# Norms for images 1 to 3 made within the first image's layer 0 scans instead of in a block of their own

## The chip, the cores and the metric

The kernel runs on one core of one Trainium2 chip. The metric is the device time of one execution in microseconds (us), median over several runs. The core has five engines with an instruction stream each: TensorE (PE in the profile; its weight loads are PEld), VectorE (DVE), ScalarE (ACT), GpSimd (POOL), and SyncE (SP), which here only issues DMAs. Each stream is in a fixed order; the engines signal to each other with semaphores. SBUF is the on-chip memory, PSUM the eight banks (128 partitions by 512 float32 each) into which TensorE writes.

## The reference

The input is x of shape (4, 384, 32, 32): four images, 384 channels, 1024 positions. Two layers follow, each a scan block and a feed-forward block, with residuals. What matters here is the beginning of layer 0, cut to its core:

```python
def _ln_c(v, eps=1e-6):                      # over the 384 channels, no scale or bias
    m = jnp.mean(v, axis=1, keepdims=True)
    s = jnp.var(v, axis=1, keepdims=True)
    return (v - m) / jnp.sqrt(s + eps)

x = x + L0_conv(_ln_c(x))                    # then the feed-forward, then layer 1

# L0_conv: four directions k (as is, turned, and both reversed), 384 channels, 16 states
dts, Bs, Cs = split(einsum('bkdl,kcd->bkcl', cross_scan(x), x_proj_weight))
dt = softplus(dt_projs_weight @ dts + bias)
h  = h * exp(dt * A) + dt * u * B            # along the 1024 positions, for each channel and state
y  = sum over states of h * C
# y + D u, directions summed, layer norm, gelu
```

## The kernel before, in words

Everything is float32. An image lies in SBUF as 128 partitions by 3 tiles by 1024 positions. Image 0 is worked alone first: its norm (`layer_norm`, L165), its layer 0 scans (`lane_scans`), and so on. The scans of images 1 to 3 begin later, and read their normed input from a DRAM tensor, `normed`. That tensor is filled by `norms_ahead` (L248 to L322), a block of its own between the norm of image 0 and its scans. It loads three images, and takes them in six halves of 512 positions. For each half TensorE sums over channels with a matrix of 1/384 (`mean_mat`), VectorE subtracts the mean, ScalarE squares, TensorE sums the squares, ScalarE makes the inverse root by Ln and Exp, and VectorE multiplies all three tiles with it (L300). SyncE stores each image. A block ends with a barrier of all engines: the scans can't begin before the last store has landed.

`lane_scans` works 12 lanes for image 0: 4 directions by 3 tiles of 128 channels. A lane has 16 steps, one for each state n. In step s the engines do this:

- ScalarE `decay` (L534): exp(delta * A) of 128 x 1024 into one of two PSUM slots (`slot(s)`, banks 2-3 or 4-5). It waits until VectorE is done with that slot, so for the product of step s-2 (or its scan).
- GpSimd `drive` (L574): du * B, up to two steps ahead of the scan.
- VectorE `scan` (L609): the recurrence over 1024 positions; it waits for decay and drive of its own step.
- the product with C: VectorE `weigh` (L618) for 11 of the 16 steps, GpSimd (L581) for n = 1, 4, 7, 10, 13 (`by_pool`), two steps later.
- TensorE `add` (L476): sums the products over n in banks 0-1 with an identity matrix. For n % 3 = 1 the add comes two steps late.

Once in each lane there is more. TensorE makes the dt product of the next lane at n = 7 (L461, banks 6-7), ScalarE turns it to softplus in three pieces at n = 10, 11, 12 (L514, L518, L522), VectorE makes `delta` at n = 12 (L597), and GpSimd `du` at n = 14 (L565). At n = 1 VectorE takes the finished sum of the lane before out of banks 0-1 (`take`: L2275, L2279 or L2283), and the first add of the new lane waits for that. When the direction changes, a projection (L450) and ScalarE's copies of it (L507) come within the last lane of a direction, with stores and loads of the B and C rows. Banks 6-7 (`WORK`) are free in the other lanes from n = 0 to n = 6. SyncE loads B rows four steps ahead (L398).

The order on each engine is written out by hand: the loop over s calls these pieces at the numbers n in the tables at the head of `lane_scans`. Nothing reorders them.

Of the kernel before, what the change touches and what calls it, by code (L numbers as in the profile page):

```python
# [17 lines left out]
ALU = mybir.AluOpType  # L18
# [8 lines left out]
P = 128  # L27
# [77 lines left out]
def load_weights(p, m, st, image):  # L105

    nc, io = p.nc, p.io
    with nc.Block() as block:
# [21 lines left out]
        def _(eng):  # L130
            eng.memset(m.eps5[:, :], 1e-5).then_inc(st.own, 1)
            eng.memset(m.eps6[:, :], 1e-6).then_inc(st.own, 1)
            eng.wait_ge(st.small, 16 * 6)

# [113 lines left out]
def norms_ahead(p, m, st, images, tiles, normed, sq, rstd, eps):  # L248


    nc, ps = p.nc, m.ps
    HALVES = len(images) * NH

    def half(j):
        return tiles[j // NH], cols(j % NH)

    with nc.Block() as block:
        @block.sync
        def _(eng):
            p.clear_last(eng, st)  # L260
            for i, x in enumerate(images):
                eng.dma_start(tiles[i], x).then_inc(st.loaded[i], 16)
            for i in range(len(images)):
                eng.wait_ge(st.normed, (i + 1) * NH)
                eng.dma_start(normed[i], tiles[i]).then_inc(st.stored, 16)
            eng.wait_ge(st.stored, 16 * len(images))

        @block.tensor
        def _(eng):
            for j in range(HALVES + 1):  # L270
                if j < HALVES:
                    t, at = half(j)
                    eng.wait_ge(st.loaded[j // NH], 16)
                    if j >= 4:
                        eng.wait_ge(st.centred, (j - 3) * CT)
                    for k in range(CT):
                        mm = eng.matmul(ps[:, j % 4, :], m.mean_mat[:, :], t[:, k, at], start=k == 0, stop=k == CT - 1)
                    mm.then_inc(st.mean, 1)
                if j:
                    v = j - 1  # L280
                    if v >= 4:
                        eng.wait_ge(st.logged, v - 3)
                    for k in range(CT):
                        eng.wait_ge(st.squared, v * CT + k + 1)
                        mm = eng.matmul(ps[:, 4 + v % 4, :], m.mean_mat[:, :], sq[:, k, cols(v % 2)], start=k == 0,
                                        stop=k == CT - 1)
                    mm.then_inc(st.variance, 1)

        @block.vector
        def _(eng):  # L290
            for j in range(HALVES + 1):
                if j < HALVES:
                    t, at = half(j)
                    eng.wait_ge(st.mean, j + 1)
                    for k in range(CT):
                        eng.tensor_tensor(t[:, k, at], t[:, k, at], ps[:, j % 4, :], ALU.subtract).then_inc(st.centred, 1)
                if j:
                    t, at = half(j - 1)
                    eng.wait_ge(st.rstd, j)
                    eng.tensor_tensor(t[:, :, at], t[:, :, at], over_tiles(rstd[:, cols((j - 1) % 2)]),  # L300
                                      ALU.mult).then_inc(st.normed, 1)

        @block.scalar
        def _(eng):
            eng.preload_act_table_set(EXP_LN)
            for j in range(HALVES + 1):
                if j < HALVES:
                    t, at = half(j)
                    if j >= 2:
                        eng.wait_ge(st.variance, j - 1)  # L310
                    for k in range(CT):
                        eng.wait_ge(st.centred, j * CT + k + 1)
                        eng.activation(sq[:, k, cols(j % 2)], t[:, k, at], ACT.Square).then_inc(st.squared, 1)
                if j:
                    v = j - 1
                    if v >= 2:
                        eng.wait_ge(st.normed, v - 1)
                    r = rstd[:, cols(v % 2)]
                    eng.wait_ge(st.variance, v + 1)
                    eng.activation(r, ps[:, 4 + v % 4, :], ACT.Ln, bias=eps[:, :]).then_inc(st.logged, 1)  # L320
                    eng.wait_ge(st.logged, v + 1)
                    eng.activation(r, r, ACT.Exp, scale=-0.5).then_inc(st.rstd, 1)  # L322


def lane_scans(p, m, st, directions, lanes, rows, turn=None, load_ahead=None):
# [17 lines left out]
    C_LATE = {1: (6,), 3: (7,)}  # L343
    prods = [m.prod[:, 0, :], m.prod[:, 1, :]]
# [38 lines left out]
    with nc.Block() as block:  # L383
        @block.sync
        def _(eng):
# [24 lines left out]

            store_rows(0)
# [6 lines left out]
            for s in range(STEPS):  # L418
                i, n = s // N, s % N
                if s + BRING < STEPS:  # L420
                    load_b(s + BRING)
                d = lanes[i].direction
# [14 lines left out]
            if load_ahead is not None:  # L437
                eng.wait_ge(st.loaded, 16)

        @block.tensor  # L440
        def _(eng):
            def project(i, c):
                d = lanes[i].direction
                x = directions[d]
                if x.turned:
                    eng.wait_ge(st.turned, CT)
                if i:
                    eng.wait_ge(st.delta, i)
                for k, src in enumerate(x.kts):
                    mm = eng.matmul(ps[0:BC + x.rank, WORK + c, :], x.wx(k), src[:, cols(c)], start=k == 0,  # L450
                                    stop=k == len(x.kts) - 1)
                mm.then_inc(st.projected, 1)

            def dt_product(i):
                x = directions[lanes[i].direction]
                eng.wait_ge(st.low, (lanes[i].direction + 1) * NH)
                if i:
                    eng.wait_ge(st.delta, i)
                a = lanes[i].dt_at
# [23 lines left out]
            for s in range(STEPS):  # L483
# [5 lines left out]
                if fresh(i + 1) and n in PROJECT_AT:  # L489
                    project(i + 1, PROJECT_AT.index(n))  # L490
                if n == DT_AT and i + 1 < len(lanes):
                    dt_product(i + 1)

        @block.scalar
        def _(eng):
            eng.preload_act_table_set(EXP_LN)

# [44 lines left out]
            for s in range(STEPS):  # L542
# [6 lines left out]
                if fresh(i + 1) and n in LOW_AT:  # L549
                    take_projection(i + 1, LOW_AT.index(n))  # L550
                if i + 1 < len(lanes):
# [40 lines left out]
        def _(eng):  # L592
# [26 lines left out]

            def take(i):  # L620
# [6 lines left out]
            for s in range(STEPS):  # L627
# [4 lines left out]
                if n == TAKE_AT and i:  # L632
                    take(i - 1)
                if n == DELTA_AT and i + 1 < len(lanes):
# [1564 lines left out]
def build(nc, io, out, rows, half_rows, normed, gates):  # L2199
    with ExitStack() as ctx:  # L2200
# [4 lines left out]
                ("x", [P, CT, L], F32), ("vec", [P, VEC_N], F32), ("ident", [P, P], F32), ("mean_mat", [P, P], F32),  # L2205
                ("eps5", [P, 1], F32), ("eps6", [P, 1], F32), ("Dsum", [P, CT], F32),
# [4 lines left out]
        def stage(name, *signals):  # L2211
# [21 lines left out]
        s_ahead = stage("ahead", "mean", "centred", "squared", "variance", "logged", "rstd", "normed", "stored",  # L2233
                        *(f"loaded{i}" for i in range(B - 1)))
        s_ahead.loaded = [s_ahead[f"loaded{i}"] for i in range(B - 1)]
# [15 lines left out]
        with ExitStack() as conv:  # L2251
# [19 lines left out]
            def first_image():  # L2271
# [9 lines left out]
                def take_turned(j):  # L2281
# [5 lines left out]
                norms_ahead(p, m, s_ahead, [io["x"][i] for i in range(1, B)], [m.h[:, :, :], ys, un], [normed[i] for i in range(1, B)],  # L2287
                            m.prod, rstd, m.eps6)
# [10 lines left out]
                with ExitStack() as scans:  # L2299
                    lane_scans(p, scan_tensors(scans, "first"), s_scan, directions, lanes, rows, turn=(u, ut))  # L2300
# [253 lines left out]
```

## Time and profile before

| | |
|---|---|
| time, median of 3 runs | 5902.71 us (5900.35 to 5903.08) |
| the profiled execution's own time | 5910.61 us, its span 5908.1 us |
| PE, DVE, ACT, POOL busy over the span | 82%, 79%, 58%, 69% |
| mean granted TensorE clock | 0.914 of full speed |
| norm of image 0, last operation ends | 30.4 us |
| block `norms_ahead` and its barrier | 30.7 to 81.5 us |
| scans of image 0 | 81.5 to about 752 us |
| the rest (layers for images 0 to 3) | about 752 to 5908 us |

All times within the trace are in us from the start of the span. A timeline row gives start, duration, engine, line, operation, and in brackets how long the engine had been idle and what ended that. Several instructions in a run are merged into one row with a count (x4). One float32 `matmul` of the kernel is two MATMUL records in the trace: the add of a step (two matmuls) is x4, a mean of a half (three matmuls) x6.

### The profile page before, as it was taken

What the parts mean: (1) busy time and instruction counts of PE and PEld (TensorE: products, weight loads), DVE (VectorE), ACT (ScalarE), POOL (GpSimd) and SP (SyncE); (2) the same over time, 40 slices, a digit from 0 to 9 for tenths busy, and PEclk for the clock granted to TensorE, in tenths of its full rate; (3) what the DMA queues carried; (4) which work ended last, traced back from release to release, by engine and by line L of the source; (5) the groups of instructions that cost most, each with busy time, mean ns of one, the idle gap of its engine ahead of it and who ended that gap; (6) DMA issues with size and microseconds to landing.
All of it is one profiled execution on the core that took longest, in us unless ns stands there. A gap on an engine that the chain in (4) does not pass through costs nothing. (4 is left out here: it accounts for less than half of the span.)

```text
span 5908.1 us, 66280 instructions
## 1 busy us (share of the span) xinstructions
PE 4843.1 (82%) x20263; PEld 3285.0 (56%) x20263; DVE 4666.1 (79%) x5015; ACT 3401.0 (58%) x5199; POOL 4054.7 (69%) x2861
## 2 busy tenths in 40 slices
PE   5777786778888897778888888778888988777998
PEld 2222242246666745656666645665766764664787
DVE  5999947969999948977999956895999984896544
ACT  3433353337777756656777756664777765664222
POOL 3999917948888817865888844893888871884121
PEclk8898898889999998888999998888999999888999
DMA  5555405428777605636777723653877761662110
GB/s 210 211 214 196 167 20 196 157 97 285 266 249 269 231 26 208 215 127 219 255 269 244 271 100 139 206 190 123 276 252 267 250 203 41 211 217 86 49 49 27
DMA packets 340470, 1076.86 MB, mean 182 GB/s; under 512 B 31522, under 2 KB 123266, under 8 KB 332808
## 3 DMA queue, kind: packets, MB, share of 16 engines
q1 hardware_dynamic: 340104, 1072.52, 52.4%
q8 instruction: 163, 2.67, 0.2%
q14 instruction: 203, 1.66, 0.1%
HBM read 1058.72 MB, written 13.68 MB: 182 GB/s over the span
## 5 line engine op out<-in xcount | busy, mean ns | idle before, releaser
L940 PE MATMUL banks<-ident,prod 128*128 128x128 f32 x4752 | 799.7, 295 | 581.8 <-DVE prod L1154 494.4
L940 PEld LDWEIGHTS banks<-ident,prod 128*128 128x128 f32 x4752 | 570.8, 149 | 906.6 <-DVE prod L1154 764.3
L476 PE MATMUL banks<-prod,ident 128*128 128x512 f32 x972 | 567.5, 725 | 299.3 <-DVE prod L618 234.6
L1141 DVE TENSOR_TENSOR_SCAN banks<-banks,h 128x512 f32<-128x512 f32 x594 | 725.7, 1222 | 99.6 <-POOL h L1092 69.4
L1092 POOL TENSOR_TENSOR h<-lane,Bb 128x512 f32<-128x512 f32 x576 | 722.5, 1273 | 51.3 <-DMA Bb<-half_rows 46.7
L1033 ACT ACTIVATE banks<-lane,A 128x512 f32<-128x512 f32 x864 | 579.5, 685 | 217.6 <-DVE prod L1154 95.2
L534 ACT ACTIVATE banks<-delta_first,A 128x1024 f32<-128x1024 f32 x288 | 321.8, 1118 | 577.2 <-DVE prod L618 479.0
L1154 DVE TENSOR_TENSOR prod<-banks,half_C_a 128x512 f32<-128x512 f32 x792 | 548.1, 692 | 98.5 <-DVE banks L1141 3.9
L1101 POOL TENSOR_TENSOR h<-h,half_C_a 128x512 f32<-128x512 f32 x360 | 461.9, 1283 | 217.4 <-DVE half_carry_a L1146 149.5
L476 PEld LDWEIGHTS banks<-prod,ident 128*128 128x128 f32 x972 | 197.1, 220 | 661.8 <-DVE prod L618 405.2
L974 PE MATMUL banks<-Cb,w_a 128*128 128x256 f32 x2304 | 552.4, 380 | 2.3 <-ACT Cb L1046 2.3
L1141 DVE TENSOR_TENSOR_SCAN banks<-banks,half_carry_a,h 128x512 f32<-128x512 f32 x396 | 506.1, 1278 | 6.6 <-POOL h L1092 3.5
L1092 POOL TENSOR_TENSOR h<-half_du_a,Bb 128x512 f32<-128x512 f32 x384 | 482.2, 1273 | 17.0 <-DMA Bb<-half_rows 15.3
L1033 ACT ACTIVATE banks<-half_delta_a,A 128x512 f32<-128x512 f32 x576 | 383.5, 684 | 161.4 <-DVE prod L1154 81.9
L609 DVE TENSOR_TENSOR_SCAN banks<-banks,h 128x1024 f32<-128x1024 f32 x198 | 453.4, 2290 | 28.0 <-POOL h L574 26.3
L961 PE MATMUL banks<-big,w_a 128*128 128x256 f32 x1728 | 443.4, 400 | 1.5 <-DMA w_a<-w_in 1.0
L974 PEld LDWEIGHTS banks<-Cb,w_a 128*128 128x128 f32 x2304 | 412.1, 190 | 45.3 <-ACT Cb L1046 3.2
L1092 POOL TENSOR_TENSOR h<-lane,Cb 128x512 f32<-128x512 f32 x288 | 364.9, 1280 | 15.9 <-DVE banks L1141 15.1
L1046 ACT ACT_TABLE_LOAD x288 | 369.5, 1283 | 5.1
L1073 ACT ACT_TABLE_LOAD x288 | 369.5, 1283 | 5.1
L574 POOL TENSOR_TENSOR h<-du_first,Cb 128x1024 f32<-128x1024 f32 x144 | 337.9, 2352 | 46.6 <-DVE h L609 21.4
L961 PEld LDWEIGHTS banks<-big,w_a 128*128 128x128 f32 x1728 | 331.3, 201 | 54.6 <-issue 11.6
(382 smaller groups left out, 10971.2 us busy)
## 6 DMA issues: line engine op xcount, KB each, us to landing
Bb<-half_rows SPq DMA_DIRECT2D x576, 512.0 KB, 4.4
Cb<-half_rows SPq DMA_DIRECT2D x288, 512.0 KB, 4.5
w_a<-w_in SPq DMA_DIRECT2D x256, 576.0 KB, 6.5
half_C_a<-half_rows SPq DMA_DIRECT2D x160, 512.0 KB, 6.6
Bb<-rows SPq DMA_DIRECT2D x144, 512.0 KB, 4.4
Cb<-rows SPq DMA_DIRECT2D x144, 512.0 KB, 4.1
w_b<-w_in SPq DMA_DIRECT2D x128, 576.0 KB, 6.4
C_first<-rows SPq DMA_DIRECT2D x40, 1024.0 KB, 8.3
```

What stands on the lines that cost most here:

```text
L476: mm = eng.matmul(ps[:, c, :], m.ident[:, :], src[:, cols(c)], start=n == 0, stop=added(s) == (i + 1) * N, skip_group_check=True)
L609: eng.tensor_tensor_scan(flip(to), flip(slot(s)), flip(m.dBu[:, s % DRIVES, :]), 0.0, ALU.mult, ALU.add).then_inc(st.scanned, 1)
L940: mm = eng.matmul(ps[:, 0, at], src[:, at], m.ident[:, :], start=n == 0 and k == 0, stop=added(s) == (i + 1) * N, is_transpose=True, skip_ ...
L961: mm = eng.matmul(hidden(u), g.w1[:, w % WRING, k, t * P:(t + 1) * P], g.un[:, k, at], start=k == 0, stop=k == CT - 1, skip_group_check=True)
L974: mm = eng.matmul(total(f), g.w2[:, w % WRING, t, f * P:(f + 1) * P], g.h[:, u % HRING, :], start=u % PER == 0 and f != 1, stop=u % PER == ...
L1033: eng.activation(slot(s), m.delta[i % 2], ACT.Exp, scale=x.A(j, n)).then_inc(st.decay, 1)
L1046: eng.activation(g.h[:, u % HRING, :], hidden(u), ACT.Gelu, bias=m.vec[:, b:b + 1]).then_inc(st.gelu, 1)
L1073: eng.preload_act_table_set(EXP_LN)
L1092: eng.tensor_tensor(m.dBu[:, s % DRIVES, :], m.du[i % 2], m.B[b % BRING][:, cols(s % 2)], ALU.mult).then_inc(st.dbu, 1)
L1101: eng.tensor_tensor(h, h, m.C[:, s % N, :], ALU.mult).then_inc(st.pooled, 1)
L1141: eng.tensor_tensor_scan(flip(to), flip(slot(s)), flip(m.dBu[:, s % DRIVES, :]), initial, ALU.mult, ALU.add).then_inc(st.scanned, 1)
L1154: eng.tensor_tensor(prods[own(s) % PRODS], slot(s), m.C[:, n, :], ALU.mult).then_inc(st.prod, 1)
```

## The change

The block `norms_ahead` is gone, and `lane_scans` gets the same work for image 0's lanes. Six of the twelve lanes, those with i = 1, 3, 4, 6, 7, 9, take one half of an image each (`norm_of`). The half is loaded into `raw` (half of the tile `un`); centring is no longer a mean on TensorE and a subtraction on VectorE, but a product with I - M and -M (`less_mean`, `minus_mean`, made once at the start of the program) that sums x minus its mean in a WORK bank. ScalarE copies it to `centred`, squares it into `raw`, and makes the inverse root; VectorE multiplies; SyncE stores. `centre` runs at n = 0, 1, 3 on TensorE, the copies at n = 1, 2, 4 and the squares at n = 4, 5, 5 on ScalarE, `variance` at n = 6 on TensorE, `inverse_root` at n = 7 on ScalarE, `normalize` at n = 9 on VectorE, and the store and the next load at n = 11 on SyncE.

```diff
+            eng.tensor_scalar(m.minus_mean[:, :], m.mean_mat[:, :], -1.0, None, ALU.mult).then_inc(st.own, 1)
+            eng.tensor_tensor(m.less_mean[:, :], m.ident[:, :], m.mean_mat[:, :], ALU.subtract).then_inc(st.own, 1)
...
-def norms_ahead(p, m, st, images, tiles, normed, sq, rstd, eps):
...
+    CENTRE_AT, CENTRED_AT, SQUARE_AT, VARIANCE_AT, RSTD_AT, NORM_AT, STORE_NORM_AT = (0, 1, 3), (1, 2, 4), (4, 5, 5), 6, 7, 9, 11
+    norm_of = {}
+    if norms is not None:
+        lanes_between = [i for i in range(1, len(lanes)) if (i + 1) % CT]
+        norm_of = {i: j for j, i in enumerate(lanes_between[:NH * len(norms.x)])}
+        raw, centred = norms.tile[:, :, cols(0)], norms.tile[:, :, cols(1)]
+        squares, rstd = raw, norms.tile[:, 0, cols(0)]
...
+            def load_x(j):
+                if j:
+                    eng.wait_ge(norms.st.normed, j)
+                eng.dma_start(raw, norms.x[j // NH][:, :, cols(j % NH)]).then_inc(norms.st.loaded, 16)
+
+            def store_norm(j):
+                eng.wait_ge(norms.st.normed, j + 1)
+                eng.dma_start(norms.to[j // NH][:, :, cols(j % NH)], centred).then_inc(norms.st.stored, 16)
...
+                if norm_of and i == 0 and n == N - 1:
+                    load_x(0)
+                if i in norm_of and n == STORE_NORM_AT:
+                    store_norm(norm_of[i])
+                    if norm_of[i] + 1 < len(norm_of):
+                        load_x(norm_of[i] + 1)
...
+            def centre(i, k):
+                j = norm_of[i]
+                if k == 0:
+                    eng.wait_ge(st.delta, i + 1)
+                    eng.wait_ge(norms.st.loaded, 16 * (j + 1))
+                if k == 2:
+                    eng.wait_ge(norms.st.centred, j * CT + 1)
+                for q in range(CT):
+                    mm = eng.matmul(ps[:, WORK + k % 2, :], (m.less_mean if q == k else m.minus_mean)[:, :], raw[:, q, :],
+                                    start=q == 0, stop=q == CT - 1)
+                mm.then_inc(norms.st.product, 1)
+
+            def variance(i):
+                j = norm_of[i]
+                for k in range(CT):
+                    eng.wait_ge(norms.st.squared, j * CT + k + 1)
+                    mm = eng.matmul(ps[:, WORK + 1, :], m.mean_mat[:, :], squares[:, k, :], start=k == 0, stop=k == CT - 1)
+                mm.then_inc(norms.st.variance, 1)
...
+                if i - 1 in norm_of:
+                    eng.wait_ge(norms.st.logged, norm_of[i - 1] + 1)
...
+                if i in norm_of and n in CENTRE_AT:
+                    centre(i, CENTRE_AT.index(n))
+                if i in norm_of and n == VARIANCE_AT:
+                    variance(i)
...
+            def take_centred(i, k):
+                j = norm_of[i]
+                if k == 0 and j:
+                    eng.wait_ge(norms.st.stored, 16 * j)
+                eng.wait_ge(norms.st.product, j * CT + k + 1)
+                eng.activation(centred[:, k, :], ps[:, WORK + k % 2, :], ACT.Copy).then_inc(norms.st.centred, 1)
+
+            def square(i, k):
+                j = norm_of[i]
+                eng.wait_ge(norms.st.centred, j * CT + k + 1)
+                eng.wait_ge(norms.st.product, (j + 1) * CT)
+                eng.activation(squares[:, k, :], centred[:, k, :], ACT.Square).then_inc(norms.st.squared, 1)
+
+            def inverse_root(i):
+                j = norm_of[i]
+                eng.wait_ge(norms.st.variance, j + 1)
+                eng.activation(rstd, ps[:, WORK + 1, :], ACT.Ln, bias=m.eps6[:, :]).then_inc(norms.st.logged, 1)
+                eng.wait_ge(norms.st.logged, j + 1)
+                eng.activation(rstd, rstd, ACT.Exp, scale=-0.5).then_inc(norms.st.rstd, 1)
...
+                if i in norm_of and n in CENTRED_AT:
+                    take_centred(i, CENTRED_AT.index(n))
+                if i in norm_of:
+                    for k in range(CT):
+                        if n == SQUARE_AT[k]:
+                            square(i, k)
+                if i in norm_of and n == RSTD_AT:
+                    inverse_root(i)
...
+            def normalize(i):
+                j = norm_of[i]
+                eng.wait_ge(norms.st.rstd, j + 1)
+                eng.wait_ge(norms.st.centred, (j + 1) * CT)
+                eng.tensor_tensor(centred, centred, over_tiles(rstd), ALU.mult).then_inc(norms.st.normed, 1)
...
+                if i in norm_of and n == NORM_AT:
+                    normalize(i)
...
-                norms_ahead(p, m, s_ahead, [io["x"][i] for i in range(1, B)], [m.h[:, :, :], ys, un], [normed[i] for i in range(1, B)],
-                            m.prod, rstd, m.eps6)
...
+                    norms = Named(st=s_ahead, tile=un, x=[io["x"][i] for i in range(1, B)], to=[normed[i] for i in range(1, B)])
+                    lane_scans(p, scan_tensors(scans, "first"), s_scan, directions, lanes, rows, turn=(u, ut), norms=norms)
+                p.last = Named(all=s_scan.all + s_ahead.all)
```

ScalarE before, from the end of lane 0 to the end of lane 1 (L534 is the decay, L547 a turned copy, L514 and L518 the next lane's softplus):

```order
L534 ACTIVATE banks<-delta_first,A 128x1024 x2
L547 ACTIVATE big<-big 128x1024
L534 ACTIVATE banks<-delta_first,A 128x1024 x12
L514 ACTIVATE du_first<-banks 128x1024
L534 ACTIVATE banks<-delta_first,A 128x1024
L518 ACTIVATE du_first<-du_first 128x1024
```

ScalarE now, lane 1 from its second decay on (L532 is the decay, L481 the copy of a centred tile, L487 the square, L492 and L494 Ln and Exp of the inverse root):

```order
L481 ACTIVATE big<-banks 128x512
L532 ACTIVATE banks<-delta_first,A 128x1024
L481 ACTIVATE big<-banks 128x512
L532 ACTIVATE banks<-delta_first,A 128x1024 x2
L481 ACTIVATE big<-banks 128x512
L487 ACTIVATE big<-big 128x512
L532 ACTIVATE banks<-delta_first,A 128x1024
L487 ACTIVATE big<-big 128x512 x2
L532 ACTIVATE banks<-delta_first,A 128x1024 x2
L492 ACTIVATE big<-banks,eps 128x512
L494 ACTIVATE big<-big 128x512
L532 ACTIVATE banks<-delta_first,A 128x1024 x3
```

The twelve decays in a row (n = 15 of lane 0, then n = 0 to 10 of lane 1) have become three ahead of the first row shown, then one, two, one, two and three, with the copies, squares and the inverse root between them.

TensorE before, from a late add of lane 0 through the dt product that lane 1 makes for lane 2 (L476 is the add, L461 the dt product):

```order
L476 MATMUL banks<-h,ident 128x512 x2
L476 MATMUL banks<-prod,ident 128x512 x12
L476 MATMUL banks<-h,ident 128x512 x2
L461 MATMUL banks<-lane,lowk 128x512 x2
L476 MATMUL banks<-prod,ident 128x512 x10
L476 MATMUL banks<-h,ident 128x512 x2
```

TensorE now, from the first add of lane 1 to its dt product (L450 is the add, L403 the centring, L411 the sum of squares, L435 the dt product):

```order
L450 MATMUL banks<-prod,ident 128x512 x2
L403 MATMUL banks<-big,less_mean 128x512
L403 MATMUL banks<-big,minus_mean 128x512 x3
L403 MATMUL banks<-big,less_mean 128x512
L403 MATMUL banks<-big,minus_mean 128x512
L450 MATMUL banks<-prod,ident 128x512 x6
L403 MATMUL banks<-big,minus_mean 128x512 x2
L403 MATMUL banks<-big,less_mean 128x512
L450 MATMUL banks<-prod,ident 128x512 x4
L450 MATMUL banks<-h,ident 128x512 x2
L411 MATMUL banks<-big,mean_mat 128x512 x3
L435 MATMUL banks<-lane,lowk 128x512 x2
```

The first two centrings (six matmuls) stand behind the first add of the lane, the third behind the adds of n = 2, 3 and 1, and the sum of squares behind the adds of n = 5, 6 and 4 and ahead of the dt product.

## Rows read from the trace of the kernel before

**Rows 1.** `windows`: stretch; us; busy of PE, PEld, DVE, ACT, POOL; clock; DMA

```profile
100.40:748.00 647.60, 465.53 (x842) 165.90 (x843) 615.21 (x346) 253.42 (x232) 607.51 (x262) 0.87 0.57 203
```

**Rows 2.** Waits by total, 100 to 740 us: total, times, longest

```profile
ACT banks L534 <- DVE prod L618: 315.8, 125, 6.4
...
DVE banks L609 <- POOL h L574: 16.6, 14, 5.0
```

**Rows 3.** Timeline of VectorE in lane 3, first half

```profile
261.87 2.30 DVE L609 TENSOR_TENSOR_SCAN banks<-banks,h 128x1024 f32<-128x1024 f32 x1 [0.96 <-POOL h L574]
...
267.63 1.26 DVE L2275 SCALAR_TENSOR_TENSOR big<-big,Dsum,banks 128x1024 f32<-128x1024 f32 x1
268.81 2.29 DVE L609 TENSOR_TENSOR_SCAN banks<-banks,h 128x1024 f32<-128x1024 f32 x1
...
274.80 1.23 DVE L618 TENSOR_TENSOR prod<-banks,C_first 128x1024 f32<-128x1024 f32 x1
...
278.13 2.27 DVE L609 TENSOR_TENSOR_SCAN banks<-banks,h 128x1024 f32<-128x1024 f32 x1
...
284.10 1.23 DVE L618 TENSOR_TENSOR prod<-banks,C_first 128x1024 f32<-128x1024 f32 x1
...
287.75 2.30 DVE L609 TENSOR_TENSOR_SCAN banks<-banks,h 128x1024 f32<-128x1024 f32 x1
```

**Rows 4.** Timeline of ScalarE, the decay of n = 2

```profile
265.56 1.12 ACT L534 ACTIVATE banks<-delta_first,A 128x1024 f32<-128x1024 f32 x1 [3.50 <-DVE prod L618]
```

**Rows 5.** Timeline of TensorE in lane 3, first half

```profile
269.04 5.46 PE L476 MATMUL banks<-prod,ident 128*128 128x512 f32 x8 [4.38 <-DVE big L2275]
276.07 3.70 PE L476 MATMUL banks<-prod,ident 128*128 128x512 f32 x8 [1.58 <-DVE prod L618]
...
285.38 2.20 PE L476 MATMUL banks<-prod,ident 128*128 128x512 f32 x4 [0.35 <-DVE prod L618]
287.42 1.88 PE L476 MATMUL banks<-h,ident 128*128 128x512 f32 x4
```

**Rows 6.** Timeline of TensorE, first add of lane 9

```profile
594.25 1.95 PE L476 MATMUL banks<-prod,ident 128*128 128x512 f32 x4 [2.63 <-DVE big L2283]
```

**Rows 7.** Timeline of all engines, the block `norms_ahead` and what follows

```profile
30.69 1.28 ACT L305 ACT_TABLE_LOAD   x1 [2.07 <-PEq L165]
...
44.46 1.82 ACT L313 ACTIVATE prod<-h 128x512 f32<-128x512 f32 x3 [12.49 <-DVE h L296]
...
48.69 2.74 PE L277 MATMUL banks<-big,mean_mat 128*128 128x512 f32 x6
...
48.89 0.69 ACT L320 ACTIVATE Cb<-banks,eps 128x512 f32<-128x512 f32 x1
...
49.61 0.63 ACT L322 ACTIVATE Cb<-Cb 128x512 f32<-128x512 f32 x1
...
50.27 1.76 DVE L300 TENSOR_TENSOR h<-h,Cb 128x1536 f32<-128x1536 f32 x1 [2.07 <-ACT Cb L322]
...
81.52 6.78 PE L450 MATMUL banks<-big,w0x 128*44 128x512 f32 x12 [8.75 <-PEq L257]
81.79 1.28 ACT L496 ACT_TABLE_LOAD   x1 [7.58 <-PEq L257]
```

**Rows 8.** Line L208: count: ns min/median/max, starts; form

```profile
L208 DVE TENSOR_TENSOR un<-un,row_all x2: 1745/2964/4182, 5457.7 to 5461.8; 128x1536 f32<-128x1536 f32 x2
```

**Rows 9.** Timeline of GpSimd around 5457 us

```profile
5455.04 5.20 POOL L1904 TENSOR_TENSOR w_lo<-raw,w_hi 128x1152 fp32r<-128x1152 f32 x2
```

**Rows 10.** Groups by line, GpSimd, 154 to 749 us

```profile
L574 POOL TENSOR_TENSOR h<-du_first,Cb 128x1024 f32<-128x1024 f32 x88 | 206.6, 2353 | 29.6 <-DVE prod L609 13.3 <-DVE h L609 13.1 <-DVE banks L609 2.6
```

**Rows 11.** DMA issues, 30 to 82 us: count, KB each, us to landing

```profile
normed<-big SPq DMA_DIRECT2D x2, 1536.0 KB, 5.1
h<-x_in SPq DMA_DIRECT2D x1, 1536.0 KB, 6.8
```

**Rows 12.** DMA issues, 100 to 740 us

```profile
Bb<-rows SPq DMA_DIRECT2D x94, 512.0 KB, 4.4
```

More of the change, by code:

```diff
@@ L245, in _ @@
                                        scale=m.vec[:, w:w + 1]).then_inc(st.scaled, 1)
-def norms_ahead(p, m, st, images, tiles, normed, sq, rstd, eps):
[L251 to L322, printed above, removed]
@@ L325, in lane_scans @@
-def lane_scans(p, m, st, directions, lanes, rows, turn=None, load_ahead=None):
+def lane_scans(p, m, st, directions, lanes, rows, turn=None, load_ahead=None, norms=None):
     nc, ps, low = p.nc, m.ps, m.low
@@ L438, in _ @@
                 eng.wait_ge(st.loaded, 16)
+            if norm_of:
+                eng.wait_ge(norms.st.stored, 16 * len(norm_of))
         @block.tensor
         def _(eng):
+            def centre(i, k):
[15 more added lines that the diff above has]
+                mm.then_inc(norms.st.variance, 1)
             def project(i, c):
@@ L2205, in build @@
                 ("x", [P, CT, L], F32), ("vec", [P, VEC_N], F32), ("ident", [P, P], F32), ("mean_mat", [P, P], F32),
+                ("minus_mean", [P, P], F32), ("less_mean", [P, P], F32),
                 ("eps5", [P, 1], F32), ("eps6", [P, 1], F32), ("Dsum", [P, CT], F32),
@@ L2232, in build @@
         s_moved = stage("moved", "sent", "reloaded")
-        s_ahead = stage("ahead", "mean", "centred", "squared", "variance", "logged", "rstd", "normed", "stored",
-                        *(f"loaded{i}" for i in range(B - 1)))
-        s_ahead.loaded = [s_ahead[f"loaded{i}"] for i in range(B - 1)]
+        s_ahead = stage("ahead", "loaded", "product", "centred", "squared", "variance", "logged", "rstd", "normed", "stored")
         s_moe = stage("moe", "ones", "got0", "got1", "scores", "step", "exped", "u_high", "u_split", "high", "split", "hidden", "gelu", "h_high", "h_split", "down",
@@ L2299, in first_image @@
                 with ExitStack() as scans:
-                    lane_scans(p, scan_tensors(scans, "first"), s_scan, directions, lanes, rows, turn=(u, ut))
+                    norms = Named(st=s_ahead, tile=un, x=[io["x"][i] for i in range(1, B)], to=[normed[i] for i in range(1, B)])
+                    lane_scans(p, scan_tensors(scans, "first"), s_scan, directions, lanes, rows, turn=(u, ut), norms=norms)
+                p.last = Named(all=s_scan.all + s_ahead.all)
             def half_scan_tensors(stack, name):
```

## The prediction

> **What bounds the kernel now.** I read first the busy shares by stretch, then the list of waits, then the timeline of one lane on each engine, because the change puts work into a loop whose order is fixed. In the scans of image 0 VectorE is busy 615.2 of 647.6 us and GpSimd 607.5; TensorE 465.5, at a mean granted clock of 0.87, and ScalarE 253.4 [rows 1]. So VectorE bounds the stage, with GpSimd just behind, and ScalarE looks as if it had room. The list of waits says what this room is made of: ScalarE stands waiting for VectorE's product 125 times, 315.8 us in all, before a decay [rows 2]. A decay writes into the slot that the product of two steps earlier has just left, and the scan after next needs it. ScalarE can't work ahead, so its idle time can't be filled with work that itself waits for something late. The timeline of lane 3 (starting at 261.87) is my example: the decay of n = 2 starts at 265.56, takes 1.12 [rows 4], and its scan starts at 268.81 [rows 3].
>
> **What goes.** The first instruction of the old block on ScalarE starts at 30.69, the same instruction of the scans at 81.79 [rows 7]. With the block gone the second moves to the place of the first: 51.1 us off. All of it is on the path, because of the barrier and because nothing of the scans ran in it. The block's loads and stores move into the scans.
>
> **What comes: the instructions.** Six lanes (i = 1, 3, 4, 6, 7, 9) get one half of an image each. On TensorE a centring is three matmuls, six passes, like the old mean of a half: 2.74 us [rows 7]; there are three per lane, and one sum of squares of the same size, 11.0 us per lane. On ScalarE: three copies and three squares of 0.61 (1.82 for three), Ln 0.69 and Exp 0.63 [rows 7]: 5.0 us per lane. On VectorE one multiplication, 1.76 [rows 7]; the subtraction is gone. By busy time alone this would cost 1.76 x 6 = 10.6 us on the bound engine. What costs is the order.
>
> **What comes: three waits per lane.** ScalarE works in its written order. A copy at n = 1 stands ahead of the decay of n = 2, and if TensorE's product isn't there the decay waits too, and VectorE behind it. I take each of the three places at which TensorE's result depends on VectorE's latest product, from the rows of lane 3.
>
> Place A, n = 0 to 2. TensorE's first centring stands behind the lane's first add, which waits for the take of the lane before; it starts at 269.04, when the take (267.63 + 1.26) is done. The row is 5.46 for eight passes, against 3.70 for eight at 276.07 [rows 5]: 1.76 more, as if the first four passes had run at 1.2 GHz after an idle time of 4.38. So the add takes 3.4, the centring 2.74, the copy 0.6, the decay 1.12, and 0.1 for signals: the scan of n = 2 starts at 277.0, not 268.81, 8.2 us late. Where TensorE is at 2.4 GHz, as in lane 9 (1.95 for four passes after 2.63 idle [rows 6]), it is 6.5. I counted the lanes' first adds: five of the six are of the slow kind, mean 7.9.
>
> Place B, n = 3 to 5. The product of n = 3 (274.80 + 1.23) releases eight passes at 276.07, two adds. The third centring can issue 3.43 later (eight times 0.43), at 279.5; 2.74, copy 0.6, square 0.6 (it is written ahead of the decay), decay 1.12, signals 0.1: 284.7, and the scan of n = 5 now starts at 278.13 [rows 3, 5]: 6.6 late.
>
> Place C, n = 6 to 8. The product of n = 6 ends at 285.33, the adds of n = 6 and 4 run from 285.38 to 289.3 [rows 3, 5]. Then the sum of squares 2.74, Ln 0.69, Exp 0.63, decay 1.12, signals and gaps 0.2: 294.6, while the scan of n = 8 starts at 287.75 now: 6.8 late.
>
> The three add up, since each chain starts from a VectorE product that comes after the stall before. Could GpSimd hide some? It runs at most two steps ahead of the scan, so it stops with VectorE. 7.9 + 6.6 + 6.8 = 21.3 us per lane. The other new pieces aren't late: the second centring is done before the decay of n = 2 is, and the squares at n = 5 stand ahead of a decay that has a whole scan and product of time.
>
> **Clock.** B and C hold 28 passes, 12 us at 2.4 GHz, and the rows I used have one slow pass between them. At the stage's mean clock of 0.87 [rows 1] they would take 1.8 more; TensorE is idle some 6 us ahead of C. I take 1.0 per lane, between 0 and 1.8.
>
> **The multiplication, and what it meets.** GpSimd is busy with operations of 2.35 [rows 10] nearly all the time. The same multiplication, with both inputs in SBUF, took 4.18 once and 1.75 once at 5457 [rows 8]; the long one began at 5457.7 and ended about when GpSimd's pair did, 5455.04 + 5.20 [rows 9]. So it waits for GpSimd's running operation: between 0 and 2.35, I take 1.2, 3.0 in all. Against this stands a gain: VectorE's 0.96 of waiting for GpSimd at a lane's first scan [rows 3] goes, since GpSimd has caught up. Net 2.0 per lane, 1.76 - 0.96 = 0.8 without the meeting, 4.1 with a full one and no gain.
>
> The Trainium skill has this as a rule: "SBUF — State Buffer", section "SBUF: two separate sides", says that a VectorE operation with two SBUF inputs and a GpSimd operation that reads SBUF exclude each other for the whole instruction. The trace agrees (4.18 beside 1.75). Without the rule one would put 0.8 in the sum, with it about 2.0: 7 us over six lanes. It speaks against the change a little; the inputs of the old subtraction and of the scan lie partly in PSUM, and were not under it.
>
> **DMA.** One store and one load of 768 KB follow each other at n = 11, behind a wait for the multiplication at n = 9. 1536 KB took 5.1 to store and 6.8 to load [rows 11], so the pair is some 6 us. Behind it in SyncE's queue are the B rows, four steps of 3.4 ahead of their use (647.6 us by 12 lanes, 54.0 each, by 16 [rows 1]), so 13 us, landing in 4.4 [rows 12]; 6 + 4.4 is less. Cost 0, and at the other end one step of 3.4 us per lane. The lanes with C loads have no store. The extra semaphores to clear and the two small matrices at the start: 0 to 1 us, taken as 0.5.
>
> **Sum.** Per lane 21.3 + 1.0 + 2.0 = 24.3; six lanes 145.8; + 0.5 - 51.1 = +95. From the profiled execution's 5910.6 that is 6006; the median of the runs shown is 7.9 below that execution, so 5902.7 + 95 = 5998 us, slower by 1.6%.
>
> **Rivals.** Slow clock: if all 34 passes of the three chains that aren't counted slow so far (6 at A, 28 at B and C, 14.6 us) ran at 1.2 GHz, it would be 14.6 instead of 1.0 per lane, +82 us: 6080. For it speaks that the stalls make TensorE's idle times longer than the 4.38 after which it was slow; against it, that eight passes at 276.07 were fast soon after. Half of it gives 6036. 5 in 100 for above 6035.
>
> Only part of the waits binds: if B and C were hidden (because ScalarE's decay turned out to be ahead of the copy, or TensorE ran the centring ahead of the adds) 7.9 + 2.0 = 9.9 per lane, +8 us: 5911. I see nothing in the order that would do it. 3 in 100.
>
> The other side: no wait binds, ScalarE's 315.8 us of waiting swallow all, and only the multiplications cost, 6 x 2.0 = 12: 12 - 51 = -39, 5864 us. It decides at the copy of n = 1: if it ends by 267.7 in lane 3 (268.81 - 1.12), nothing is lost there. Since even at 2.4 GHz TensorE can't begin the centring before 270.7, I give it 3 in 100. That the block is not really on the path, or that the scans stay where they are, would need work in it that the scans share; there is none.
>
> DMA: B rows late by a step in each of six lanes, +20: 6018. 6 in 100, inside the range.
>
> **Range and chances.** The lowest sum of the forecast has every pass at 2.4 GHz (A 6.5, B 6.5, C 6.5), 0.8 for the multiplication, and 1.7 us saved at the first projection, which now runs its first passes slow after 8.75 idle [rows 7]: 6 x 20.3 - 51 - 1.7 = +69, 5972. The highest has half of the slow clock, 6036. I say 5972 to 6035. A measurement of this kernel can tell about 0.2%, 12 us, from no change. Faster by more than that: 3 in 100. Within: 4 in 100. Slower: 93 in 100.
>
> **What would show it.** In the profile after: ScalarE waits for TensorE ahead of the copies of n = 1 and n = 4 and ahead of Ln at n = 7; VectorE's scans of n = 2, 5 and 8 wait for a decay, some 8, 7 and 7 us, in six lanes, and nowhere else; these lanes last about 78 us instead of 54. The multiplication takes over 1.76 where GpSimd is busy. The first scan comes 51 us earlier. I am wrong if these scans start on time, or if lanes with a half last under 70 us.

## The result, and the profile after

The changed kernel takes 6011.5 us in the median (6007.2 to 6016.0, 4 runs), the kernel before 5902.9: a ratio of 1.0181, 95% interval 1.0168 to 1.0194. Five more runs of it, in a later set with its own runs of before, had a median of 6006.25 against 5910.0, ratio 1.0164 (1.0150 to 1.0178). It is slower by 1.6 to 1.8%, where +1.6% was forecast.

The profiled execution lasted 6007.2 us with a span of 6005.4, which is 97.3 more than before. Three marks divide it: the first scan of image 0, the first DMA of the stage behind the scans, and the end.

| profile | first scan starts | scans of image 0 | later stages |
|---|---|---|---|
| before | 100.4 | 652.1 | 5155.6 |
| changed | 47.2 | 803.1 | 5155.1 |
| difference | -53.2 | +151.0 | -0.5 |

The stage of the scans, to hold against [rows 1]:

```profile
47.23:846.10 798.87, 560.85 (x988) 206.12 (x989) 631.40 (x352) 277.83 (x280) 608.95 (x262) 0.83 0.49 177
```

VectorE's busy time is 631.4 against 615.2, which is little for a stage that is 151 longer. The bound engine has become idle. The list of waits from 50 to 800 us (engine and line that waited, what it waited for, total, times, longest), to hold against [rows 2]:

```profile
ACT banks L532 <- DVE prod L624: 226.7, 100, 6.4
...
ACT big L481 <- PE banks L403: 142.3, 18, 14.3
DVE banks L615 <- ACT banks L532: 133.1, 18, 9.1
...
ACT big L492 <- PE banks L411: 55.2, 6, 10.1
...
DVE banks L615 <- POOL h L580: 11.3, 18, 1.0
```

VectorE waited 18 times for a decay, three times in each of six lanes, 133.1 us in all; before there was no such line. ScalarE's own waiting for VectorE's product is down from 315.8 to 226.7, and beside it stand 142.3 for the centred product and 55.2 for the sum of squares. VectorE's waits for GpSimd have hardly changed: the 11.3 here and the 16.6 of [rows 2] differ mainly by the first scan's 4.95, which this window leaves out. Lane 3 on VectorE, against [rows 3]:

```profile
234.04 2.30 DVE L615 TENSOR_TENSOR_SCAN banks<-banks,h 128x1024 f32<-128x1024 f32 x1 [0.95 <-POOL h L580]
...
250.14 2.30 DVE L615 TENSOR_TENSOR_SCAN banks<-banks,h 128x1024 f32<-128x1024 f32 x1 [9.07 <-ACT banks L532]
...
265.89 2.30 DVE L615 TENSOR_TENSOR_SCAN banks<-banks,h 128x1024 f32<-128x1024 f32 x1 [6.33 <-ACT banks L532]
...
282.21 2.30 DVE L615 TENSOR_TENSOR_SCAN banks<-banks,h 128x1024 f32<-128x1024 f32 x1 [6.91 <-ACT banks L532]
...
289.34 2.83 DVE L630 TENSOR_TENSOR big<-big 128x1536 f32<-128x1536 f32 x1
```

The bracket before the scans of n = 2, 5 and 8 reads 9.07, 6.33 and 6.91, and the last row is the multiplication, 2.83. Over the six lanes the three waits average 8.7, 6.5 and 7.0. From first scan to first scan these lanes last 78.9 us on average (77.5 to 81.0), where they lasted 54.0. ScalarE in the same lane, against [rows 4]:

```profile
248.51 0.60 ACT L481 ACTIVATE big<-banks 128x512 f32<-128x512 f32 x1 [14.26 <-PE banks L403]
249.00 1.11 ACT L532 ACTIVATE banks<-delta_first,A 128x1024 f32<-128x1024 f32 x1
...
263.73 0.60 ACT L481 ACTIVATE big<-banks 128x512 f32<-128x512 f32 x1 [8.78 <-PE banks L403]
264.23 0.62 ACT L487 ACTIVATE big<-big 128x512 f32<-128x512 f32 x1
264.74 1.11 ACT L532 ACTIVATE banks<-delta_first,A 128x1024 f32<-128x1024 f32 x1
...
279.82 0.69 ACT L492 ACTIVATE big<-banks,eps 128x512 f32<-128x512 f32 x1 [9.12 <-PE banks L411]
280.54 0.63 ACT L494 ACTIVATE big<-big 128x512 f32<-128x512 f32 x1
281.07 2.14 ACT L532 ACTIVATE banks<-delta_first,A 128x1024 f32<-128x1024 f32 x2
```

Each copy or Ln ends a long wait for TensorE, and a decay (L532) stands right behind it: that decay is the one VectorE waited for. TensorE, against [rows 5]:

```profile
241.22 3.75 PE L450 MATMUL banks<-prod,ident 128*128 128x512 f32 x4 [4.37 <-DVE big L2288]
244.76 1.91 PE L403 MATMUL banks<-big,less_mean 128*128 128x512 f32 x2
246.47 2.80 PE L403 MATMUL banks<-big,minus_mean 128*128 128x512 f32 x6
...
269.60 5.89 PE L450 MATMUL banks<-prod,ident 128*128 128x512 f32 x8 [5.90 <-DVE prod L624]
275.33 1.88 PE L450 MATMUL banks<-h,ident 128*128 128x512 f32 x4
277.04 2.74 PE L411 MATMUL banks<-big,mean_mat 128*128 128x512 f32 x6
```

The first add takes 3.54 us for its four passes (241.22 to 244.76) after 4.37 idle, so it runs at 1.2 GHz, and the first two passes of the centring are slow too (1.71 to 246.47); the next six take 2.63. At 269.60 the add of n = 5 begins after 5.90 us of idleness and is slow again, up into the adds ahead of the sum of squares.

### The profile page after: what moved, and what is told of

Its sections match the earlier page's. It is cut to its first block and busy times, and to the rows that moved or that the text cites. A ratio compares the mean times of both kernels' runs of the same rounds, so it can differ in the third digit from the quotient of the medians.

```text
span 6005.4 us, 66441 instructions
## 1 busy us (share of the span) xinstructions
PE 4899.9 (82%) x20335; PEld 3306.1 (55%) x20335; DVE 4659.0 (78%) x4999; ACT 3406.1 (57%) x5216; POOL 4059.7 (68%) x2861
## 5 line engine op out<-in xcount | busy, mean ns | idle before, releaser
L450 PE MATMUL banks<-prod,ident 128*128 128x512 f32 x972 | 601.2, 764 | 346.6 <-DVE prod L624 277.7
L450 PEld LDWEIGHTS banks<-prod,ident 128*128 128x128 f32 x972 | 209.5, 235 | 728.5 <-DVE prod L624 457.2
L532 ACT ACTIVATE banks<-delta_first,A 128x1024 f32<-128x1024 f32 x288 | 321.0, 1116 | 507.1 <-DVE prod L624 412.2
L615 DVE TENSOR_TENSOR_SCAN banks<-banks,h 128x1024 f32<-128x1024 f32 x198 | 453.3, 2289 | 160.6 <-ACT banks L532 133.1
L580 POOL TENSOR_TENSOR h<-du_first,Bb 128x1024 f32<-128x1024 f32 x144 | 337.4, 2351 | 96.3 <-DVE banks L615 59.2
```

What stands on the lines that cost most here:

```text
L450: mm = eng.matmul(ps[:, c, :], m.ident[:, :], src[:, cols(c)], start=n == 0, stop=added(s) == (i + 1) * N, skip_group_check=True)
L580: eng.tensor_tensor(m.dBu[:, s % DRIVES, :], m.du[:, i % 2, :], m.B[s % BRING], ALU.mult).then_inc(st.dbu, 1)
L615: eng.tensor_tensor_scan(flip(to), flip(slot(s)), flip(m.dBu[:, s % DRIVES, :]), 0.0, ALU.mult, ALU.add).then_inc(st.scanned, 1)
```

## The experiments

Stage times are from each kernel's profile, as in the table above. e1 to e4 and e5 to e8 were timed in two sets, each beside its own runs of before (medians 5906.55 and 5910.03), so across the sets the ratios compare better than the medians.

| kernel | median us | ratio to before, 95% | first scan | scans | later |
|---|---|---|---|---|---|
| e1 no norms | 5864.9 | 0.9929, 0.9916 to 0.9942 | 50.7 | 654.0 | 5158.7 |
| e2 one step later | 5952.0 | 1.0076, 1.0063 to 1.0088 | 50.9 | 738.9 | 5158.9 |
| e3 A in front | 5955.9 | 1.0091, 1.0076 to 1.0106 | 47.5 | 750.5 | 5153.0 |
| e4 all in front | 5885.6 | 0.9969, 0.9957 to 0.9981 | 51.0 | 676.8 | 5149.6 |
| e5 multiplication at n = 10 | 5873.0 | 0.9938, 0.9925 to 0.9952 | 46.6 | 661.5 | 5166.7 |
| e6 root in PSUM | 5877.0 | 0.9944, 0.9930 to 0.9957 | 47.9 | 667.0 | 5171.4 |
| e7 changed again | 6006.3 | 1.0164, 1.0150 to 1.0178 | 46.5 | 802.9 | 5155.1 |
| e8 8 columns | 5870.2 | 0.9941, 0.9927 to 0.9955 | 46.7 | 666.9 | 5154.8 |

**e1: no norms.** The call of the scans without the norms, and images 1 to 3 entering un-normed:

```diff
-                    lane_scans(p, scan_tensors(scans, "first"), s_scan, directions, lanes, rows, turn=(u, ut), norms=norms)
+                    lane_scans(p, scan_tensors(scans, "first"), s_scan, directions, lanes, rows, turn=(u, ut))
-            from_scans("first", following=normed[1])
+            from_scans("first", following=io["x"][1])
```

> Left out: the norms of images 1 to 3, in either form; these images enter layer 0 as they are loaded. This prices the removed block alone. If the block and its barrier were wholly on the path (my theory), the first scan starts near 47 us instead of 100.4, and the time is before's 5903 less 52 to 53, so 5850, with every lane at 54.0 us. If part of the block had hidden something (a cold TensorE, late B rows), less than 45 us would go.

Measured: 5864.9, which is 41.6 us under before, not 52, and under the 45 that I had named as the sign that the block had hidden something. The profile doesn't show that. The profiled execution is 44.7 shorter than before's: the first scan comes 49.7 earlier, the scans are 1.9 longer and the later stages 3.1. The 1.9 are at the very end, where VectorE's last `take` waits 5.87 for TensorE instead of 3.79; the changed kernel has that too (5.99). The other 3.1 lie between the profiled executions and the medians. The first scan is at 50.7 and not at 47.2 as in the changed kernel: 0.8 because this execution came to the first projection later, and 2.7 because TensorE worked more slowly in it; first e1, then the changed kernel:

```profile
30.58 7.99 PE L422 MATMUL banks<-big,w0x 128*44 128x512 f32 x12 [3.50 <-PEq L167]
```

```profile
29.82 5.32 PE L422 MATMUL banks<-big,w0x 128*44 128x512 f32 x12 [3.50 <-PEq L167]
```

The same twelve passes after the same idle time took 7.99 in one execution and 5.32 in the other. And the first scans:

```profile
50.67 2.30 DVE L615 TENSOR_TENSOR_SCAN banks<-banks,h 128x1024 f32<-128x1024 f32 x1 [4.95 <-POOL h L580]
```

```profile
47.23 2.30 DVE L615 TENSOR_TENSOR_SCAN banks<-banks,h 128x1024 f32<-128x1024 f32 x1 [4.95 <-POOL h L580]
```

So the first scan comes 50 to 53 us earlier without the block. That the missing 8 us of the median are differences between executions (below), and not something that the block had hidden, is the likelier reading; these runs don't prove it.

**e2: ScalarE one step later.**

```diff
-    ... = (0, 1, 3), (1, 2, 4), (4, 5, 5), 6, 7, 9, 11
+    ... = (0, 1, 3), (2, 3, 5), (5, 6, 6), 6, 8, 9, 11
```

> ScalarE's pieces one step later than in the changed kernel: copies at n = 2, 3, 5, squares at 5, 6, 6, inverse root at 8; TensorE's and VectorE's orders unchanged. If the cost is ScalarE's order, each stalled decay gains one scan and one product of VectorE (3.57 us): per lane 8.7, 6.5, 7.0 become 5.1, 3.0, 3.4, so 10.7 x 6 = 64 us less than the changed kernel, about 5945. If instead the cost is the amount of added work (TensorE's passes or ScalarE's 5 us per lane), the same work stays and so does the time: 6010.

Measured: 5952.0, and scans 64.2 us shorter than in the changed kernel. Lane 1 on VectorE, the three waits:

```profile
119.30 2.30 DVE L615 TENSOR_TENSOR_SCAN banks<-banks,h 128x1024 f32<-128x1024 f32 x1 [4.41 <-ACT banks L532]
...
131.48 2.30 DVE L615 TENSOR_TENSOR_SCAN banks<-banks,h 128x1024 f32<-128x1024 f32 x1 [2.78 <-ACT banks L532]
...
145.59 2.30 DVE L615 TENSOR_TENSOR_SCAN banks<-banks,h 128x1024 f32<-128x1024 f32 x1 [4.71 <-ACT banks L532]
```

They were 9.14, 6.33 and 7.00 in that lane. B gained 3.55, just a scan and a product; A 4.7, since the decay of n = 2 is now ahead of the first copy and the wait is at n = 3. C gained only 2.3 here: the add of n = 6 now begins right at its product, after 4.19 us without work (135.19), and takes 3.5 us for its four passes, 1.3 more than in the changed kernel, where the slow passes came earlier. All 18 together: 71.4 instead of 133.1. The work is the same to the instruction, so its amount isn't what costs.

**e3: the first two centrings ahead of the first add.**

```diff
+                if i in norm_of and n == 0:
+                    centre(i, 0)
+                    centre(i, 1)
                 if not by_pool(s):
                     add(s)
...
-                if i in norm_of and n in CENTRE_AT:
-                    centre(i, CENTRE_AT.index(n))
+                if i in norm_of and n == CENTRE_AT[2]:
+                    centre(i, 2)
...
-                if norm_of and i == 0 and n == N - 1:
+                if norm_of and i == 0 and n == N - 3:
```

> Only wait A treated: the first two centrings stand ahead of the lane's first add on TensorE (which waits for VectorE's take) instead of behind it; the first load is two steps earlier. Order theory: the wait before the scan of n = 2 (8.7 us on average) goes, the other two stay, 52 us less: about 5958. TensorE works through its idle time of 4.4 us, so that its first add runs at 2.4 GHz. Rival (the decay of n = 2 is late for another reason, or the added TensorE work makes the add late enough to stop VectorE): under 30 us gained.

Measured: scans 52.6 shorter, 5955.9 against 5958 expected. Waits for decays are down from 133.1 to 82.2; at place A only two remain, of 1.3 us, in lanes 3 and 7. In lane 1 two waits are left:

```profile
123.73 2.30 DVE L618 TENSOR_TENSOR_SCAN banks<-banks,h 128x1024 f32<-128x1024 f32 x1 [6.33 <-ACT banks L535]
...
139.71 2.30 DVE L618 TENSOR_TENSOR_SCAN banks<-banks,h 128x1024 f32<-128x1024 f32 x1 [6.56 <-ACT banks L535]
```

TensorE in that lane goes from the adds of the lane before into the centring with no idle row, and the first add of the lane (108.73) takes 1.88 for four passes, at 2.4 GHz:

```profile
101.86 1.88 PE L450 MATMUL banks<-h,ident 128*128 128x512 f32 x4
103.58 1.02 PE L403 MATMUL banks<-big,less_mean 128*128 128x512 f32 x2
104.44 2.74 PE L403 MATMUL banks<-big,minus_mean 128*128 128x512 f32 x6
...
108.73 1.88 PE L450 MATMUL banks<-prod,ident 128*128 128x512 f32 x4
```

**e4: all three.** The edit of e3, and

```diff
-    ... = (0, 1, 3), (1, 2, 4), (4, 5, 5), 6, 7, 9, 11
+    ... = (0, 0, 0), (1, 2, 4), (4, 4, 5), 5, 8, 9, 11
```

> All three waits treated: as the one before, with the third centring right behind the first add, squares at n = 4, 4, 5, the sum of squares at n = 5 and the inverse root at n = 8. Order theory: no scan waits for a decay; what is left of the norms is VectorE's multiplication, 2.8 us in six lanes. So the time without norms (5850) plus 17: about 5868, 0.6% faster than before. If the amount of work on TensorE or the lower clock costs by itself, the time stays over 5885.

Measured: 5885.6, faster than before by 0.3%, but 18 us over the 5868 that I expected, and just inside what I had given to the rival (that the added work or the clock costs by itself). 15 of the 18 are in the base: e1 took 5864.9 where I had put 5850. The rest is in the scans, which are 22.8 longer than without norms, where I had put 17. The waits for decays are gone but for one of 1.3 us, so the order theory holds. The multiplication has grown: 3.89 us in the median, not 2.83. VectorE, then GpSimd:

```profile
136.38 1.23 DVE L627 TENSOR_TENSOR prod<-banks,C_first 128x1024 f32<-128x1024 f32 x1
137.52 3.90 DVE L633 TENSOR_TENSOR big<-big 128x1536 f32<-128x1536 f32 x1
141.34 2.28 DVE L618 TENSOR_TENSOR_SCAN h<-banks,h 128x1024 f32<-128x1024 f32 x1
```

```profile
135.13 4.67 POOL L583 TENSOR_TENSOR h<-du_first,Cb 128x1024 f32<-128x1024 f32 x2
```

GpSimd's second operation began at about 137.44, the multiplication at 137.52, and it ended at 141.42, 1.6 after GpSimd's end at 139.80.

**e5: the multiplication at n = 10.** The edit of e4 with 10 for 9.

> As front_all, but VectorE's multiplication stands at n = 10, right behind a scan whose product is GpSimd's, instead of at n = 9 behind VectorE's product. In front_all it took 3.90 us, because GpSimd's next operation had begun 0.1 us before it. Exclusion theory (while GpSimd's operation runs, a VectorE operation with two SBUF inputs waits): at n = 10 VectorE issues it as the scan ends, ahead of GpSimd, which waits for that scan; it takes 1.76, and GpSimd starts 1.6 later. Time about 12 us under front_all's 5886, so 5874. If the length comes from something else (its six-way stride, ScalarE writing nearby), it stays near 3.9 and the time at 5886.

Measured: 5873.0, as expected. The scans are 15.3 shorter than e4's. The medians are 12.6 apart, or 16 when each is held against the before of its own set.

```profile
133.16 2.29 DVE L618 TENSOR_TENSOR_SCAN h<-banks,h 128x1024 f32<-128x1024 f32 x1
135.37 1.73 DVE L633 TENSOR_TENSOR big<-big 128x1536 f32<-128x1536 f32 x1
137.02 2.29 DVE L618 TENSOR_TENSOR_SCAN banks<-banks,h 128x1024 f32<-128x1024 f32 x1
```

```profile
135.59 3.71 POOL L583 TENSOR_TENSOR h<-du_first,Bb 128x1024 f32<-128x1024 f32 x1 [0.20 <-DVE h L618]
139.26 2.35 POOL L590 TENSOR_TENSOR h<-h,C_first 128x1024 f32<-128x1024 f32 x1
```

Now VectorE is first by 0.2 us. The multiplication takes 1.73, and GpSimd's operation beside it 3.71 instead of 2.35. In e4 and here, the one that starts second waits for the other to end. This version beats both kernels, before by 0.6%.

**e6: the inverse root in PSUM.** The edit of e4, and

```diff
-        squares, rstd = raw, norms.tile[:, 0, cols(0)]
+        squares, rstd = raw, ps[:, WORK + 1, :]
...
-                if i - 1 in norm_of:
-                    eng.wait_ge(norms.st.logged, norm_of[i - 1] + 1)
+                if i - 1 in norm_of:
+                    eng.wait_ge(norms.st.normed, norm_of[i - 1] + 1)
```

with the dt product at n = 9, and softplus, `delta` and `du` one step later in the six lanes.

> As front_all, but the inverse root is left in PSUM (bank 7), so that the multiplication reads one input from SBUF and one from PSUM; it stands at n = 9 as there. The next lane's dt product waits for it (n = 9), and its softplus, delta and du are one step later in six lanes. Exclusion theory: 1.76 us, however GpSimd stands, 13 us less in six lanes, minus up to 1 us per lane for the later du: 5873 to 5880. Rival: still 2.8 to 3.9 us, and no gain.

Measured: 5877.0. The multiplication stands where e4 has it, beside a running GpSimd operation:

```profile
133.31 1.22 DVE L627 TENSOR_TENSOR prod<-banks,C_first 128x1024 f32<-128x1024 f32 x1
134.45 1.74 DVE L633 TENSOR_TENSOR big<-big,banks 128x1536 f32<-128x1536 f32 x1
```

```profile
132.05 4.67 POOL L583 TENSOR_TENSOR h<-du_first,Cb 128x1024 f32<-128x1024 f32 x2
```

GpSimd works from 132.05 to 136.72, and the multiplication takes 1.74 in the midst of it, in all six lanes (1742 to 1744 ns). With one input in PSUM there is no waiting on either side: GpSimd's pair takes its usual 4.67. Of the 12.9 us so won (six times 3.89 - 1.74), 9.8 show in the scans. The other 3 are lost to waits that e4 doesn't have: 0.36 for a decay in each of the six lanes, and 1.4 instead of 0.96 for GpSimd before the first scan behind five of them, probably because of the later `du`.

**e7: the changed kernel again.**

> The changed kernel itself again, beside the others on one chip. Its profiled execution lasted 97 us longer than before's, its median 109. If the stages behind image 0's scans are untouched, their length agrees with before's within the spread between executions (5150 to 5159 us in six profiles), and the median of more runs comes to 5906 + 97 = 6003. If something in the later stages is slower by the change, the median stays 109 above before.

Measured: 6006.25, 96.2 above the before of its runs, with scans of 802.9 and later stages of 5155.1. So nothing in the later stages is slower by the change.

**e8: 8 of 1536 columns multiplied.** The edit of e4, and

```diff
-                eng.tensor_tensor(centred, centred, over_tiles(rstd), ALU.mult).then_inc(norms.st.normed, 1)
+                eng.tensor_tensor(centred[:, 0, 0:8], centred[:, 0, 0:8], rstd[:, 0:8], ALU.mult).then_inc(norms.st.normed, 1)
```

> As front_all, but of the multiplication only 8 of 1536 columns are made (left out: nearly all of the scaling of images 1 to 3). All TensorE and ScalarE work, all DMAs and all semaphores stay. If only the multiplication costs in front_all, this takes what the kernel without norms took: 5865, with image 0's scans 654 us long from the first scan to the end. If the 11 us of TensorE and 5 us of ScalarE per lane cost by themselves, 5875 or more.

Measured: 5870.2, but the scans took 666.9, not 654. My expectation missed that the small operation has two SBUF inputs too:

```profile
L633 DVE TENSOR_TENSOR big<-big x6: 2273/2297/2314, 133.3 to 578.7; 128x8 f32<-128x8 f32 x6
```

2.3 us for 8 columns is nearly all waiting for GpSimd, and six times that is 13.8. Between 666.9 and 654.0 lie 12.9, but e1's stage ends with 2.1 us of waiting for TensorE that e8's doesn't have (5.87 against 3.79), so some 15 is the fair difference. What the 13.8 leave over is 1.2, and the trace has it: one wait of 1.19 for a decay, in lane 3. The other work, 11 us of TensorE and 5 of ScalarE per lane, costs nothing that shows in the other five lanes, where nobody waits for it. The 3.89 of e4 is these 2.3 plus the 1.6 of work.

**How executions differ.** The later stages are the same instructions in all ten profiles, and took 5149.6 to 5171.4. Twenty-one more runs of before lay between 5898.4 and 5916.2. Differences of this size are enough for what is missing in e1's median, and for the changed kernel being +109 in one set of runs and +96 in the other. I didn't find out what sets them. TensorE's speed differs in places from one execution to the next, as in the first projection above. Over the later stages TensorE was busy 4310 us in the shortest (e4) and 4336 and 4330 in the two longest (e5, e6), with VectorE the same within 3; but e8 had 4327 in a stage of ordinary length (5154.8). So the cause of the 22 us stays open.

## Why the prediction was right, step by step

- *What bounds the stage, and that ScalarE's room isn't free.* Right. e2 and e4 keep the same work in another order and take 64 and 126 us off the scans.
- *What goes: 51.1.* 53.2 in the profile after. TensorE's first projection starts 51.7 earlier (29.82 against 81.52), 0.9 of which is that the norm of image 0 ended earlier in this execution, and it is 1.5 shorter, at 2.4 GHz throughout (5.32 against 6.78 [rows 7]). e1 and e4, where it was slow, had 49.7 and 49.4, so the 2.1 above the forecast are luck.
- *Place A: 7.9.* 8.7. The add was slow as said; I let the centring run at full speed behind it, but its first two passes were slow too, 0.9 us more. Lane 9, fast before, was slow here (8.98).
- *Place B: 6.6.* 6.5; 6.33 in five lanes, with TensorE at 2.4 GHz.
- *Place C: 6.8* (its terms add up to 6.9). 7.0. Here the clock came in, after 5.90 us without work, and partly hid behind the product of n = 6.
- *Clock, 1.0 per lane.* All in all 22.2 of waiting per lane (133.1 by 6) against 21.3 + 1.0. Right as a sum, but I had put the clock's share at B and C, and it was nearly all in A.
- *The multiplication: 3.0, of which 0.96 comes back.* 2.83, of the kind of [rows 8, 9], but next to nothing came back. This is the term that was mis-sized: the six lanes are 24.9 longer on average, of which 22.2 is waiting for decays, so the net is 2.7 and not 2.0. I argued that GpSimd had caught up. It had, but its lead is two steps at most, and at the scan of n = 10 it stands waiting for VectorE in both kernels. From there it works through eight operations without a pause, up to the one that the next lane's first scan needs, and that takes as long as before: 18.6 us from its start behind the scan of n = 10 (297.36 before, 294.52 now) to that first scan (315.99, 313.13). What GpSimd had gained was gone ahead of that. GpSimd before:

```profile
297.36 2.36 POOL L574 TENSOR_TENSOR h<-du_first,Bb 128x1024 f32<-128x1024 f32 x1 [0.20 <-DVE h L609]
```

VectorE now, the last scan of lane 3 and the first of lane 4; the row of GpSimd at 294.52 stands below:

```profile
308.51 2.30 DVE L615 TENSOR_TENSOR_SCAN banks<-banks,h 128x1024 f32<-128x1024 f32 x1 [0.15 <-POOL h L580]
...
313.13 2.30 DVE L615 TENSOR_TENSOR_SCAN banks<-banks,h 128x1024 f32<-128x1024 f32 x1 [0.96 <-POOL h L580]
```

- *DMA: 0.* Right: no wait for B rows shows in the list.
- *Sum: +95.* +97.3 between the profiles, +109 and +96 between medians. Part of the closeness is luck, since misses cancel: 2.1 more went than forecast; against it stand 4 more for the multiplication in six lanes, and 1.7 outside these lanes, mostly in the last one, where TensorE's last eight passes took 5.90 instead of 3.70. The rivals of a slow clock throughout (+177) and of waits that don't bind (-39) are both out; the forecast's own range, 5972 to 6035, held both medians.

The multiplication's lines in the changed kernel:

```profile
L630 DVE TENSOR_TENSOR big<-big x6: 2828/2832/2842, 156.1 to 712.6; 128x1536 f32<-128x1536 f32 x6
```

```profile
288.21 2.35 POOL L580 TENSOR_TENSOR h<-du_first,Cb 128x1024 f32<-128x1024 f32 x1 [1.21 <-DVE banks L615]
294.52 2.35 POOL L580 TENSOR_TENSOR h<-du_first,Bb 128x1024 f32<-128x1024 f32 x1 [3.96 <-DVE h L615]
```

GpSimd's operation at 288.21 ends at 290.56, the multiplication (289.34 + 2.83) at 292.17, 1.6 later. It was the same at 5457 in the kernel before, where the prediction reads [rows 8, 9] a little loosely: the long multiplication ended at 5461.9, not about when GpSimd's pair did (5460.2) but 1.6 after it, about its own working time. e5, e6 and e8 show the mechanism, which the prediction had from one pair of rows and from the Trainium skill ("SBUF — State Buffer", section "SBUF: two separate sides"). The rule of mutual exclusion holds here: VectorE waited for GpSimd in e4 (3.89), GpSimd for VectorE in e5 (3.71 instead of 2.35), and 8 columns waited like 1536 in e8. The changed kernel's trace alone could not have told it from an operation that is slow for its access pattern.

## What to carry to other kernels

An engine's idle time is a place for new work only if the work is ready when it comes up in that engine's order. For each inserted instruction ask what it waits for, and what stands right behind it. ScalarE was idle more than half the time and each of three insertions cost 6 to 9 us. One place later on ScalarE alone brought about half of that back (e2). Nearly all of it came back when the products were also made earlier, where TensorE idles anyway, ahead of the add that waits, and the inverse root stood later (e4).

A VectorE operation with two SBUF inputs beside a busy GpSimd is placed where GpSimd has just been released by VectorE itself, or gets one operand from PSUM.

## What the runs showed of the hardware that I had not expected

- A multiplication of 8 columns took 2.3 us, as long as GpSimd's operation beside it: the wait doesn't depend on the size. In place of 3.89, the full one took 1.73 when VectorE issued it 0.2 us ahead of GpSimd, and 1.74 with one input in PSUM.
- The same twelve passes after the same 3.50 us of idle time ran in 5.32 in one execution and 7.99 in another, so TensorE's clock at that place differs between executions.
- Identical later stages differ by up to 22 us of 5150 between executions (0.4%), more than the scatter of the first three runs of before (2.7 us) suggests; later runs of before lay 18 us apart.
